# q, k and attention recast: three terms on row pairs, projections already turned, products with v of two key blocks together at every second block

## The reference

```python
x = x + 0.5 * ffn(layernorm(x))
x = x + attention(layernorm(x))
x = x + 0.5 * ffn(layernorm(x))

# ffn: h = relu(x @ W_fc.T) ** 2 (1024 hidden), y = h @ W_proj.T,
#      five steps of mem = 0.9 * mem + y - (mem > 1); the share of steps with mem > 1
# attention: 16 heads of D = 16; q, k = x @ W.T, each rotated by position (pairs 2i, 2i+1:
#      r1 = t1 * cos - t2 * sin, r2 = t1 * sin + t2 * cos);
#      softmax(q k^T / 4, causal) @ (x @ Wv.T + bv), then @ Wo.T + bo
```

## Time and profile before

| | |
|---|---|
| median of 3 runs | 1724.12 us (1723.69 to 1725.47) |
| the profiled execution | 1728.13 us, its span 1726.4 us |
| mean granted PE clock | 0.933 of full speed |
| first phase / attention / third phase | 0 to 411.6 / to 1468 / to 1726.4 us |
| busy | PE 1505.3 us (87%), PEld 828.1, DVE 1200.0 (70%), ACT 947.9 (55%), POOL 353.9 (21%) |
| moved by DMA | 90.54 MB, mean 52 GB/s |

### The profile page before, as it was taken

The page is one execution under the profiler, slowest core; times in us unless marked ns, Lnnn a source line. Parts: engine busy times, 40 slices in busy tenths (PEclk is TensorE's granted clock), DMA queues, the critical chain, the costliest instruction groups (busy, mean ns, idle before and its releaser), DMA issues. The chain is left out here.

```text
span 1726.4 us, 32516 instructions
## 1 busy us (share of the span) xinstructions
PE 1505.3 (87%) x11104; PEld 828.1 (48%) x11104; DVE 1200.0 (70%) x2269; ACT 947.9 (55%) x1332; POOL 353.9 (21%) x378
## 2 busy tenths in 40 slices
PE   5989888671489999998999989999999999599997
PEld 4877777551123333332333333333333333499996
DVE  4687766740478888886888877877887880366776
ACT  5656666562015555554555645555555568266654
POOL 0046656896001011011011020020010101101000
PEclk9999989885559999999999999999999999699999
DMA  4112222326352042052051070060150000322221
GB/s 117 60 39 71 83 73 74 105 79 122 37 62 32 5 62 36 5 73 26 5 79 19 5 94 5 5 93 5 19 81 6 4 8 5 111 74 86 97 73 62
DMA packets 130140, 90.54 MB, mean 52 GB/s; under 512 B 50625, under 2 KB 126401, under 8 KB 129985
## 3 DMA queue, kind: packets, MB, share of 16 engines
q1 hardware_dynamic: 104640, 75.92, 22.3%
q10 hardware_dynamic: 25344, 12.59, 2.4%
HBM read 54.53 MB, written 33.55 MB: 51 GB/s over the span
## 5 line engine op out<-in xcount | busy, mean ns | idle before, releaser
L983 DVE TENSOR_REDUCE maxes<-m_ps 128x1 f32<-128x512 f32 (+3 forms) x1280 | 743.6, 608 | 220.5 <-PE m_ps L1069 113.1
L963 ACT ACTIVATE probs<-s_ps 128x1024 f32<-128x1024 f32 (+3 forms) x640 | 540.8, 894 | 390.6 <-PE s_ps L1101 389.5
L1066 PE MATMUL m_ps<-kT,qT 96*128 96x512 bf16 (+3 forms) x1280 | 457.7, 369 | 102.3 <-DVE maxes L983 45.4
L1121 PE MATMUL o_ps<-probs,v_w 128*32 128x256 f32 (+2 forms) x4352 | 345.9, 393 | 0.3 <-POOL probs L936 0.3
L1101 PE MATMUL s_ps<-qT,kT 99*128 99x512 bf16 (+3 forms) x1280 | 341.1, 352 | 2.1 <-ACT probs L963 1.7
L1066 PEld LDWEIGHTS m_ps<-kT,qT 96*128 96x128 bf16 x1280 | 122.3, 97 | 443.4 <-DVE maxes L983 279.3
L936 POOL TENSOR_SCALAR_AFFINE_SELECT probs<-probs 128x512 f32<-128x512 f32 x128 | 81.3, 635 | 936.7 <-ACT probs L963 936.7
L1101 PEld LDWEIGHTS s_ps<-qT,kT 99*128 99x128 bf16 x1280 | 109.7, 99 | 107.1 <-issue 27.0
L1121 PEld LDWEIGHTS o_ps<-probs,v_w 128*32 128x32 f32 x4352 | 87.5, 108 | 132.5 <-issue 119.7
L1069 PE MATMUL m_ps<-maskb,identb_b 128*128 128x128 bf16 x512 | 116.6, 230 | 0.0
L520 POOL TENSOR_TENSOR prod_a<-qk_a,cosb_a 128x256 f32<-128x256 f32 x64 | 69.5, 1085 | 168.1 <-ACT qk_a L343 167.9
(11 more groups left out here) (138 smaller groups left out, 2228.1 us busy)
## 6 DMA issues: line engine op xcount, KB each, us to landing
qkT_parts<-qkT_a ACTq DMA_DIRECT2D x48, 256.0 KB, 2.9
qT<-qkT_parts SPq DMA_DIRECT2D x192, 64.0 KB, 4.5
kT<-qkT_parts SPq DMA_DIRECT2D x48, 256.0 KB, 6.0
xin_a<-in_x SPq DMA_DIRECT2D x8, 512.0 KB, 4.2
xres_a<-in_x SPq DMA_DIRECT2D x8, 512.0 KB, 5.2
x<-xsum_a SPq DMA_DIRECT2D x8, 512.0 KB, 4.4
v_tok<-v_a SPq DMA_DIRECT2D x8, 512.0 KB, 3.0
v_in<-v_tok SPq DMA_DIRECT2D x8, 512.0 KB, 7.2
```

Of the source, the lines that this page charges most:

```text
L963: act.activation(probs[:, b % PBUF, 2 * hp:2 * hp + 2, off:CH], s_ps[hp][:, :, off:CH], ACT.Exp)\
L983: dve.tensor_reduce(maxes[:, j % 2, h, t, k:k + 1], m_ps[:, u % 2, 0:width], AX.X, ALU.max)\
L1066: mm = pe.matmul(m_ps[:, u % 2, 0:width], q, kT[dn % 2][0:KR, h, k * CH:k * CH + width], start=True, stop=(k < j))
L1121: mm = pe.matmul(o_ps[VW * h:VW * (h + 1), start:end], v_w[dn % 2][:, b, h, :], probs[:, b % PBUF, h, start:end], start=(b == 0), stop=(b ...
```

## The change

- **Parts.** q and k are stored as float32 in two parts (high, low). Three products (high x high, high x low, low x high) of 16 rows: 48 rows per head and 2 rows for the maximum, in fp32r. The four heads of a group lie as two pairs, one head of a pair in rows 0 to 63, the other in rows 64 to 127 (HR).
- **Projection.** `project_pair` computes q (x = 0) or k (x = 1) transposed, features on partitions, 512 tokens wide, the even and the odd element of each rotated pair in one half of gps each. DVE `turn_pair` multiplies both by the tables (2 operations of 1024 columns), POOL `rotate` adds and subtracts (512 each) and makes the low part (1024), ACT `part_high` the high part, and SP stores (4 DMAs per part of q or k). `rope`, `part`, `fill` and the bf16 identity are gone. v comes from `project_v` in one piece. The stages stand one iteration earlier, in new steps f; the loops of both feed-forward phases are written out. The table is one load of 3 MB.
- **Attention.** The mask is no longer added by PE: on the diagonal DVE adds it and takes the maximum in one tensor_tensor_reduce, which writes the masked tile too and has one more wait. `negate` has four operations, its last a DVE transpose of 32 x 32 blocks straight into shiftT; `turn_max` and `send` are gone; `shift` is 16 DMAs. `load` has six DMAs per term, one term at each j. Rows of ones for both kT are memsets of 32 rows x 4096 (DVE for the first, POOL for the second), and SP waits for them, and for a memset of the mask, before it loads.
- **Order.** The products with v are made for a whole block (512 queries), for two blocks together, at odd b, with nothing between; at even b there are none. ACT's exp now applies the scale 1/4.

The diff, cut to its core:

```diff
-QS, KS = (0, 0, 1, 1, 0, 2), (0, 1, 0, 1, 2, 0)
+
+QS, KS = (0, 0, 1), (0, 1, 0)
 NT = len(QS)
 KR = NT * D
-KC = KR + 3
+KC = KR + 2
...
+                        if f == 1 and has(3):
+                            part_high(it - 3, 0)
+                        if f == 2 and has(2):
+                            std("mid", it - 2, mln)
+                        if f == 4 and has(3):
+                            v_evac(it - 3)
+                        if f == 5 and has(2):
+                            high("mid", it - 2, mT_hi)
+                        if f == 6 and has(3):
+                            part_high(it - 3, 1)
...
+            def turn_pair(c, x):
+
+                wait(dve, "proj_done", 3 * c + x + 1)
+                wait(dve, "rot_done", 4 * c + 2 * x)
+                if c == 0 and x == 0:
+                    wait(dve, "table_in", 16)
+                    wait(dve, "w_lo", 3)
+                t0 = c * CH % S
+                for m in range(2):
+                    dve.tensor_tensor(turned[:, m], gps[:, :, :], table[:, m:m + 2, t0:t0 + CH], ALU.mult)\
+                       .then_inc(s["turn_done"], 1)
...
+                    if first and f == 5 and has(2):
+                        low("mid", it - 2, mT_hi, mT_lo)
...
+                    if first and f == 1 and has(2):
+                        wait(dve, "sum_done", it - 1)
+                        norm_stats("mid", it - 2, xsum, mstats, mmv, mln)
+                    if first and f == 2 and has(3):
+                        turn_pair(it - 3, 1)
                     if f == (3 if first else 4) and has(-1):
                         norm("pre", it + 1, xin if first else x2, xn, mv, ln)
+                    if first and f == 3 and has(2):
                         norm("mid", it - 2, xsum, xm, mmv, mln)
+                    if first and f == 7 and has(2):
+                        turn_pair(it - 2, 0)
...
+            def rotate(c, x):
+
+                n = 4 * c + 2 * x
+                wait(pool, "turn_done", n + 2)
+                wait(pool, "part_hi", 2 * (c - 1) + x + 1)
+                wait(pool, "part_lo", 2 * (c - 1) + x + 1)
+                for m, op in enumerate((ALU.subtract, ALU.add)):
+                    pool.tensor_tensor(rot[:, x, m, :], turned[:, m, 0, :], turned[:, m, 1, :], op)\
+                        .then_inc(s["rot_done"], 1)
+                wait(pool, "part_hi", 2 * c + x + 1)
+                wait(pool, "rot_done", n + 2)
+                wait(pool, f"qk_out{x}", 64 * c)
+                pool.tensor_tensor(qk_lo[:, x, :, :], rot[:, x, :, :], qk_hi[:, x, :, :].bitcast(F32), ALU.subtract)\
+                    .then_inc(s["part_lo"], 1)
...
+            def project_pair(c, x):
+
+                if x == 0:
                     wait(pe, "mid_evac", c + 1)
-                if i % 2 == 0:
-                    wait(pe, "v_evac", T * c + t)
-                    project(gps[:, 0, :], t, 0, 2 * E).then_inc(s["qk_done"], 1)
+                    wait(pe, "v_evac", c)
                 else:
-                    wait(pe, "qk_evac", T * c + t + 1)
-                    project(gps[:, 0, 0:E], t, 2 * E, 3 * E).then_inc(s["v_done"], 1)
+                    wait(pe, "turn_done", 4 * c + 2)
+                for ab in range(2):
+                    n0 = (2 * x + ab) * P
+                    for i, (wt, x_, k) in enumerate([(a, b, k) for k in range(EC) for a, b in
+                                                     ((proj_hi, mT_hi), (proj_hi, mT_lo), (proj_lo, mT_hi))]):
+                        last = pe.matmul(gps[:, ab, :], wt[:, k, n0:n0 + P], x_[:, k, :],
+                                         start=(i == 0), stop=(i == 3 * EC - 1))
+                last.then_inc(s["proj_done"], 1)
...
+                    if first and f == 0 and has(3):
+                        project_pair(it - 3, 1)
+                    if first and f == 3 and has(3):
+                        project_v(it - 3)
+                    if first and f == 4 and has(2):
+                        wait(pe, "mid_norm", it - 1)
+                        turn(xm, "mid_T")
+                    if first and f == 6 and has(2):
+                        project_pair(it - 2, 0)
...
-        UNITS = [(j, t, h, k, CH if k < j else P * (t + 1))
-                 for j in range(NJ) for t in range(T) for h in range(G) for k in range(j + 1)]
+        UNITS = [(j, t, 2 * hp + par, k, CH if k < j else P * (t + 1))
+                 for j in range(NJ) for t in range(T) for hp in range(G // 2) for k in range(j + 1) for par in range(2)]
...
+            sp.wait_ge(mask_ok, 1)
+            sp.dma_start(mask[:, CH - P:CH], w["mask"]).then_inc(const_in, 16)
...
             def load(i, dn, terms):
-                tok, row = place(i, dn)
+                tok, group = place(i, dn)
                 p = dn % 2
                 for m in terms:
-                    q, k = (io["qkT"][a, bass.ds(row + first, G * D), bass.ds(tok, S)] for a, first in
-                            ((QS[m], 0), (KS[m], E)))
-                    for j in range(NJ):
-                        sp.dma_start(qT[p][D * m:D * (m + 1), j, :, :],
-                                     q[:, j * CH:(j + 1) * CH].rearrange("(h d) t -> d h t", d=D))\
+                    for par in range(2):
+                        rows = slice(HR * par + D * m, HR * par + D * (m + 1))
+                        keys = io["qkT"][KS[m], 1].rearrange("(g hp par d) t -> g d par hp t", g=NG, hp=G // 2, par=2)
+                        sp.dma_start(kT[p][rows, :, :].bitcast(F32), keys[bass.ds(group, 1), :, par, :, bass.ds(tok, S)])\
                           .then_inc(qk_in[p], 16)
-                    sp.dma_start(kT[p][D * m:D * (m + 1), :, :], k.rearrange("(h d) t -> d h t", d=D))\
-                      .then_inc(qk_in[p], 16)
+                        for hp in range(G // 2):
+                            queries = io["qkT"][QS[m], 0].rearrange("(g hp par d) t -> g hp par d t", g=NG, hp=G // 2, par=2)
+                            sp.dma_start(qT[p][rows, :, hp, :].bitcast(F32),
+                                         queries[bass.ds(group, 1), hp, par, :, bass.ds(tok, S)]
+                                         .rearrange("g d (j c) -> (g d) j c", c=CH)).then_inc(qk_in[p], 16)
...
-                    sp.dma_start(qT[dn % 2][KR + a:KR + a + 1, j, :, :],
-                                 shiftT[a * G * T:(a + 1) * G * T, :]).then_inc(shift_in, 16)
+                for a in range(2):
+                    for par in range(2):
+                        row = HR * par + KR + a
+                        out = qT[dn % 2][row:row + 1, j, :, :].rearrange("o h (t r n) -> o (h t) r n", t=T, r=P // VW)
+                        for r in range(P // VW):
+                            c0 = VW * r + G * T * a + G * T // 2 * par
+                            sp.dma_start(out[:, :, r, :].bitcast(F32), shiftT[c0:c0 + G * T // 2, :]).then_inc(shift_in, 16)
...
+                    if j == 0 and (dn == 0):
+                        wait(sp, ones_ok[1], 2)
                     if j == 0 and (dn > 0):
 
                         sp.wait_ge(s_done, exp_units(n, 0, 0))
                         sp.wait_ge(v_ready, n)
-                    load(i, dn + 1, (2 * j, 2 * j + 1))
+                    load(i, dn + 1, (j,))
...
-            dve.memset(negparts[:, :, :], 0.0).then_inc(neg_zero, 1)
-            dve.wait_ge(neg_zero, 1)
+
+            for par in range(2):
+                dve.memset(kT[0][HR * par + HR // 2:HR * (par + 1), :, :].bitcast(F32), 1.0).then_inc(ones_ok[0], 1)
+            dve.memset(mask[:, :], 0.0).then_inc(mask_ok, 1)
+            dve.wait_ge(const_in, 32)
 
             def unit(i, dn, u):
 
                 n = 2 * i + dn
                 j, t, h, k, width = UNITS[u]
                 dve.wait_ge(max_done, len(UNITS) * n + u + 1)
-                dve.tensor_reduce(maxes[:, j % 2, h, t, k:k + 1], m_ps[:, u % 2, 0:width], AX.X, ALU.max)\
-                   .then_inc(max_read, 1)
+                out = maxes[:, j % 2, 2 * (h % 2) + h // 2, t, k:k + 1]
+                if k < j:
+                    dve.tensor_reduce(out, m_ps[:, u % 2, 0:width], AX.X, ALU.max).then_inc(max_read, 1)
+                else:
+
+                    dve.wait_ge(max_read, FREE_M + len(UNITS) * n + u - 1)
+                    dve.sem_inc(passed_max, 1)
+                    dve.tensor_tensor_reduce(masked[:, u % 2, 0:width], m_ps[:, u % 2, 0:width], mask[:, CH - width:CH], 1.0, NEG,
+                                             ALU.add, ALU.max, out).then_inc(max_read, 1)
...
+                    dve.wait_ge(neg_step, 3 * t + 3)
+                    wait(dve, shift_in, SHIFTS * t)
+                    dve.transpose(shiftT[:, :], negparts[:, :, :].rearrange("p a c -> p (a c)").bitcast(F32))\
+                       .then_inc(neg_out, 1)
...
-                q = qT[dn % 2][0:KR, j, h, t * P:(t + 1) * P]
-                mm = pe.matmul(m_ps[:, u % 2, 0:width], q, kT[dn % 2][0:KR, h, k * CH:k * CH + width],
```

(93 more changed lines are left out.)

386 lines of the change are left out of this document (122 added, 264 removed).

## The result

The changed kernel takes **2078.06 us** (median, 2075.13 to 2082.96) against 1724.39 us before on the same chip: a ratio of 1.2053, 95% interval 1.2027 to 1.2079. The prediction was 1752, range 1666 to 1830. The direction was right and the size off by an order: +28 forecast, +354 measured.

A forecast was written before the change was run, and what follows sets the result against it. PE was taken to bound a 120.48 us head group, DVE second. Phase 1 -47, attention start +8.5, seven groups +59.5, last group +9.5, phase 3 -2: +28.5 on 1728.1, 1756.6, median 4 lower: 1752; range 1666 to 1830.

The forecast's parts named there:

- The step that failed: Steady head group: PE waits more, so 4.5 us per group for stretches at 1.2 GHz, giving 129 us per group.
- the clock sinks often: Rival, chance 0.14: a third of the time at 1.2 GHz makes a head group 138 us, the kernel 1826.
- low all along: Clock low throughout: PE's work doubles past DVE's, a head group reaches 180 us, the kernel 2100; outside the range.
- The masked reduce's extra: Attention's 64 diagonal units per group: writing the accumulator costs 0.08 us each, between 0 and 0.167, 5 us per group.
- DVE idle in bursts: Head group: DVE idle 1.14 us in each of 20 bursts (two blocks' products with nothing between), 23 us per group.
- A pair of heads: Attention on PE: a pair's two matmuls priced at 0.32 us against 0.43 before, between 0.22 and 0.43.
- The last group: Last head group, without maxima: ACT gets no new scores during a double product of 2 us, +9.5 us (0 to 20).
- The start of attention: SP's load waits for DVE's two memsets of 3.5 us each and the mask's: +8.5 us (ends -5 and +12).
- The shift rows: Attention: 16 small DMAs instead of three take 9.5 us plus 1.7 to land, for j=3 hidden, barely.
- Phase 1: First feed-forward phase: chunks of 41.5 us with two new PE waits, ending near 364 instead of 411.6: -47 us.
- the tail: End of the first phase, after the last yps copy: 48 us against 90.7, counting nothing for hops between engines.
- the maxima keep pace: Rival, chance 0.33: DVE idles under 0.9 us per burst, a group at or below 118 us, the kernel 1668.

The follow-up runs named there:

- before_find_48: The kernel before with its finds (PE's matmuls for the maxima) contracting 48 rows instead of 96, all else the same: 2380.09 us (2317.22 to 2492.33), from 1724.76.
- after_zero_rows: The changed kernel with each head's q in its own tile, zero in the other head's rows, so finds and scores contract 128 rows: 1865.86 us, ratio 1.0811.

## Why the prediction was wrong

**The step that failed** is the clock: "I take 4.5 us per group for stretches at 1.2 GHz". It was reached from stretches in which PE waits, and the rival "the clock sinks often" gave a third of the time at 1.2 GHz. The profile shows 0.66, two thirds of the time. The case that comes nearest in its number (low all along, a group of 180, 2100 us) was named and put outside the range, and it too had only the waits as its reason. The cause was not among my reasons at all. I asked what makes PE idle; the experiments show that PE busy 98% runs at half clock when 160 of its matmuls use 48 rows instead of 96, and at 0.97 to 1.00 with the same columns over all 96. Halving the rows stood in the diff as a saving. before_find_48 shows it with one thing changed. after_zero_rows shows the way back, with the overlap of pairs gone as well. Whether it is the rows in use or the changes between half and full tiles was not separated.

The Trainium skill (TensorE: Matmul & The Clock Gate, "What's actually happening") says that a monitor sets the clock by how busy PE has lately been. By the rows here that is not enough: 226.51 of 230.01 us busy at 0.50. In this kernel busy must be read with the rows of the matmuls.

**A head group, term by term.** DVE's work, 95 forecast: 98.05. The masked reduce's extra, 0.08 taken between 0 and 0.167: 0.083, in an instruction of its own.

```profile
L948 DVE DVE_READ_ACCUMULATOR2_ANT maxes<- 128x1 f32 x512 | 42.5, 83 | 0.0
```

The Trainium skill's two instructions (VectorE: DVE Perf Modes, "Two Vector instructions with no wait between them") are there, at half the price that I gave them. DVE idle in bursts, 20 x 1.14 = 23: 20 gaps, as said, but 52.8 us, 2.64 each, since most products run at half clock; at full clock 1.58 was seen, so 1.14 was low too. The smaller gaps, 6.5: 12.0. Together with 4.7 of other idle time that is 167.56. The number of gaps and their mechanism were right; their price hung on the clock.

**A pair of heads** was priced at 0.32 us between 0.22 and 0.43. It is the lower end: two finds of a pair that start together, both places of m_ps being free, take 0.79 at half clock, what one takes (792.49 and 796.97 above). The Trainium skill (TensorE: Matmul & The Clock Gate, "Measured speedup vs the span model") had that right, and the trace agrees. It was taken to bring the group down by 1 to 2 us; in this kernel that saving is lost in the clock.

**The last group**, +9.5 forecast: +38.9, with its clock at 0.71 where it was 1.00. **The start of attention**, +8.5: 9.4 to the first maximum, with DVE's two memsets of 3.47 us as estimated and a first read at 437.32, 45.7 us after the phase's start (36.3 before); to the first exp it is 14.5. **The shift rows** were hidden, as forecast. **Phase 3**: +1.2 instead of -2.

**Phase 1**, -47 forecast: -20. The waits came where they were put: 4.1 for turned (4.3 forecast) and up to 3.9 for y_a (2.8). A chunk took 44.7 instead of 41.5, the very pace of the kernel before, and the tail 60 instead of 48. The tail's terms add up to 46.3, not to the 48 that the prediction states, so it was short by 13.7. One mis-sized term is visible, DVE's passes of 1024 columns, which I took at 1.22 everywhere. Those with tps or the tables do take 1.22; those on y_a average 1.63 (1.40 in the kernel before):

```profile
L390 DVE SCALAR_TENSOR_TENSOR count_a<-y_a,count_a 128x1024 bf16<-128x1024 f32 x32 | 52.0, 1626 | 0.1
```

while the same passes of the third phase take 1.219. The cause is open; POOL's share of busy time doesn't explain it, for from 95 to 302 us it is 25% here and was 61% before, with the shorter passes.

**The rival of the other side** (the maxima keep pace, 1668) fell: DVE idles far over 0.9 us per burst. Its decision point, 122 us per group, was never near. The chance of 0.14 on the clock was the real mistake in weighing.

## What to carry to other kernels

Before a change packs fewer rows into a matmul, or runs two small ones at once, ask what the granted clock rests on. It can cost more than the whole saving, and filling up with zero rows can be the faster kernel (1866 against 2078 us here). An experiment that changes only the rows is two lines and answers it; PE's busy share doesn't. And where a change has parts, price them apart: here the projection's redesign was a gain hidden under attention's loss, and one wait of 4 us per chunk, read from PE's timeline, was worth 2% when its step was moved.

## What the runs showed of the hardware

- The granted clock of a steady group fell with the contracted rows at equal columns, order and type: 96 rows in the finds 0.97 to 1.00, 48 rows 0.50 to 0.93 from group to group. The changes between half and full tiles rose with it.
- Rows in which one operand is zero are enough: 0.94 to 0.99 where the kernel without them, and with pairs at once, had 0.66 to 0.68.
- With the finds on 48 rows the time is unsteady: 2317 to 2492 us between executions of before_find_48, where the kernel before stays within 0.3%.
- Two matmuls on rows 0 to 63 and 64 to 127 ran fully at once where they started together (at half clock 0.79 for two, 0.79 for one), but going from a full tile to a half one or back costs PE time at full clock (find to scores 0.43 us against 0.24 in fp32r, 0.32 against 0.22 in bf16).
